# State delta of a chunked delta-rule attention kernel: 32-row parts of the turned keys in place of zero-padded key copies

## What is computed

```python
s = s * alpha[..., None]
u = jnp.einsum('bhd,bhdv->bhv', kt, s)
s = s - beta[..., None] * jnp.einsum('bhd,bhv->bhdv', kt, u)
s = s + beta[..., None] * jnp.einsum('bhd,bhv->bhdv', kt, vt)
out = jnp.einsum('bhdv,bhd->bhv', s, qt)
```

## Time and profile before

| | us |
|---|---|
| runs | 1864.84, 1876.25, 1890.15 |
| median of the runs | 1876.25 |
| the profiled execution's own time | 1873.82 |
| its span, first to last instruction | 1871.8 |
| PE busy | 1449.1 (77%) |
| DVE busy | 1274.1 (68%) |
| ACT busy | 634.8 (34%) |
| POOL busy | 360.1 (19%) |

### The profile page before, as it was taken

One profiled execution on the slowest core, in us unless ns is written; L12 is line 12 of the kernel. 1 busy time (PEld: TensorE's weight loads), 2 busy tenths in 40 slices (PEclk: granted clock), 3 DMA queues, 4 the chain that ended last, 5 costly groups with the idle time before them and its releaser, 6 DMA issues. The chain is left out here.

```text
span 1871.8 us, 46841 instructions
## 1 busy us (share of the span) xinstructions
PE 1449.1 (77%) x18540; PEld 946.9 (51%) x18568; DVE 1274.1 (68%) x3341; ACT 634.8 (34%) x1342; POOL 360.1 (19%) x515
## 2 busy tenths in 40 slices
PE   1687988797878887787879786888869897974685
PEld 0343664365525653465436562566436663652665
DVE  5568576966787667866796578765695678534564
ACT  4430243223422262134312352124312442222564
POOL 1210141014201320015101420023001420110232
PEclk8568996899689987998789979896699968996898
DMA  8980001010010001000100001000101000102223
GB/s 252 322 254 18 8 8 30 2 23 20 8 23 21 5 20 29 18 8 19 30 13 12 20 8 23 21 5 19 30 11 19 13 14 12 24 26 99 69 70 125
DMA packets 128139, 81.97 MB, mean 44 GB/s; under 512 B 75185, under 2 KB 118513, under 8 KB 127922
## 3 DMA queue, kind: packets, MB, share of 16 engines
q1 hardware_dynamic: 124466, 69.94, 13.6%
q0 software_dynamic: 3456, 8.95, 1.5%
HBM read 27.72 MB, written 51.15 MB: 42 GB/s over the span
## 5 line engine op out<-in xcount | busy, mean ns | idle before, releaser
L789 POOL COPY kx<-kend_t 32x256 f32<-32x256 f32 x256 | 114.3, 447 | 807.3 <-PE ps L1349 787.5
L1286 PE MATMUL ps<-wv,ident 128*128 128x512 f32 x320 | 173.7, 676 | 10.6 <-DVEq L1654 10.5
L1729 DVE SCALAR_TENSOR_TENSOR state<-state,gam,ps 128x128 f32<-128x128 f32 x512 | 137.4, 339 | 49.1 <-PE ps L1349 49.1
L1673 DVE TENSOR_TENSOR nv<-ps,nrm 128x512 f32<-128x512 f32 x64 | 44.2, 691 | 175.9 <-PE ps L1209 175.4
L1349 PE MATMUL ps<-w,kx 128*64 128x128 f32 x2048 | 127.1, 277 | 0.0
L1643 DVE TENSOR_TENSOR nv<-kq,kq_blk 128x31 f32<-128x31 f32 (+15 forms) x248 | 113.7, 458 | 16.7 <-ACT mem L852 10.8
L1349 PEld LDWEIGHTS ps<-w,kx 128*64 128x64 f32 x2048 | 111.7, 138 | 12.9 <-issue 12.9
L1521 DVE TENSOR_TENSOR kq_leaf<-kq,eleaf 128x1024 f32<-128x1024 f32 x32 | 39.9, 1247 | 112.6 <-ACT kq L882 112.4
L1286 PEld LDWEIGHTS ps<-wv,ident 128*128 128x128 f32 x320 | 66.7, 218 | 94.0 <-issue 77.5
L233 PE MATMUL ps<-eleaf,wf 128*128 128x512 f32 x112 | 62.0, 681 | 50.9 <-DVEq L1654 31.8
L999 ACT ACTIVATE w<-ps 128x512 f32<-128x512 f32 x64 | 38.2, 597 | 173.8 <-PE ps L1307 173.8
(11 more groups left out here) (313 smaller groups left out, 3303.9 us busy)
## 6 DMA issues: line engine op xcount, KB each, us to landing
slot_d<-row SPq DMA_DIRECT2D x16, 2064.0 KB, 20.3
xin<-slot_d SPq DMA_DIRECT2D x39, 129.0 KB, 2.1
a_d<-yt SPq DMA_DIRECT2D x8, 512.0 KB, 2.6
kq_blk<-a_d SPq DMA_DIRECT2D x32, 128.0 KB, 2.8
u_d<-kq SPq DMA_DIRECT2D x8, 512.0 KB, 2.6
ub<-u_d SPq DMA_DIRECT2D x128, 32.0 KB, 1.9
wall<-in_w SPq DMA_DIRECT2D x8, 512.0 KB, 7.9
xt<-in_xT POOLq DMA_DIRECT2D x8, 256.0 KB, 3.4
```

The source lines that it names most:

```text
L789: m = pool.tensor_copy(kx[part, :, b4, :], kend_t[part, g, 2 * q:2 * q + 2, :])
L1286: pe.matmul(bw.t[:, :], ident[:, :], wv[:, 0:512], start=True, stop=True)
L1729: k = dve.scalar_tensor_tensor(out=state[:, hp, b, :], in0=state[:, hp, b, :], scalar=gam[:, hp, b:b + 1], in1=bd[j].t[:, DV * x:DV * x + ...
```

## The change

The buffer `kx`, its clearing by ACT, its semaphore and the 256 copies by POOL are gone. PE multiplies 32 rows of `kend_t` by the same 32 rows of `w`: 16 products of 32 rows by 64 columns for each tile, in two halves. A half takes two sequences, which lie in two row groups of the array and go to the two banks; between the halves PE waits for `row_step`. The waits that went through `kx_ready` now name the delta banks: ACT's copy of `w` waits for both banks of the tile before, the overwriting of `kend_t` for the last tile of the chunk before, and POOL's `early_differences` for tile 5. POOL's body no longer waits for `xsum_ready`, which it had raised itself.

```diff
-    kx = sb("kx", [P, 2, GB, P])
...
@@ gpsimd body
-            for i in range(TILES):
-                g, q = i // 2, i % 2
-                if nxt and i == TILES - 1:
-                    pool.wait_ge(kx_ready.sem, kx_ready.at(c, TILES - 1))
-                    early_differences(nxt, c)
-                    pool.wait_ge(d_ready.sem, d_ready.at(nxt, 2))
...
-                for j in range(2):
-                    if i:
-                        pool.wait_ge(bd[j].full.sem, bd[j].filled(c, f"d{i - 1}"))
...
-                for b4 in range(GB):
-                    part = slice(CH * b4, CH * b4 + CH)
-                    m = pool.tensor_copy(kx[part, :, b4, :], kend_t[part, g, 2 * q:2 * q + 2, :])
-                m.then_inc(kx_ready.sem, 1)
+            for j in range(2):
+                pool.wait_ge(bd[j].full.sem, bd[j].filled(c, f"d{TILES - 3}"))
+            settle(c)
             if nxt:
-                pool.wait_ge(kx_ready.sem, kx_ready.at(c, TILES))
+                early_differences(nxt, c)
                 keep_h(nxt, c)
             if last:
-                pool.wait_ge(kx_ready.sem, kx_ready.at(c, TILES))
                 pool.wait_ge(zeroed, 16 * ZFILL)
                 head_on_pool(pool, last, room, "scatter", lambda: settle(c))
@@ scalar: ends_turned, body, first
-                act.wait_ge(kx_ready.sem, kx_ready.at(c, TILES, 1))
+                for j in range(2):
+                    act.wait_ge(bd[j].full.sem, bd[j].filled(c, f"d{TILES - 1}", 1))
...
-                        act.wait_ge(bd[1].full.sem, bd[1].filled(c, f"d{i - 1}"))
+                        for j in range(2):
+                            act.wait_ge(bd[j].full.sem, bd[j].filled(c, f"d{i - 1}"))
...
-            act.activation(kx[:, :, :, :].rearrange("p a b v -> p (a b v)"), zero(2 * GB * P),
-                           ACT.Copy).then_inc(s_cleared, 1)
@@ tensor body
-                    pe.wait_ge(kx_ready.sem, kx_ready.at(c, i + 1))
                     settle(c)
-                    for b4 in range(GB):
+                    for half in range(2):
+                        if half:
+                            m.then_inc(row_step, runs.next())
+                            pe.wait_ge(row_step, runs.n)
                         for j in range(2):
                             for h2 in range(2):
-                                o = DV * (2 * (b4 // 2) + j)
-                                m = pe.matmul(bd[b4 % 2].t[DK * h2:DK * h2 + DK, o:o + DV],
-                                              kx[:, j, b4, DK * h2:DK * h2 + DK], w[:, 2 * j + h2, :],
-                                              start=True, stop=True)
-                        if b4 >= 2:
-                            m.then_inc(bd[b4 % 2].full.sem, 1)
+                                for x in range(2):
+                                    b4, o = 2 * half + x, DV * (2 * half + j)
+                                    part, keys_of = slice(CH * b4, CH * b4 + CH), slice(DK * h2, DK * h2 + DK)
+                                    m = pe.matmul(bd[x].t[keys_of, o:o + DV], kend_t[part, g, 2 * q + j, keys_of],
+                                                  w[part, 2 * j + h2, :], start=True, stop=True)
+                                    if half and j and h2:
+                                        m.then_inc(bd[x].full.sem, 1)
```

More of the change, by code:

```diff
@@ L575, in attention @@
     row_step = sem("row_step")
-    pace, kx_ready = sig("pace", PACES), sig("kx_ready", TILES)
+    pace = sig("pace", PACES)
     beta_step, norm_step = sig("beta_step", 8), sig("norm_step", 7)
@@ L765, in body @@
                 head_on_pool(pool, last, room, "xsum", lambda: settle(c))
-            if last:
-                pool.wait_ge(hd.xsum_ready.sem, hd.xsum_ready.at(last, 1))
-            for i in range(TILES):
-                g, q = i // 2, i % 2
-                if nxt and i == TILES - 1:
-                    pool.wait_ge(kx_ready.sem, kx_ready.at(c, TILES - 1))
-                    early_differences(nxt, c)
-                    pool.wait_ge(d_ready.sem, d_ready.at(nxt, 2))
[L775 to L780, removed]
-                for j in range(2):
-                    if i:
-                        pool.wait_ge(bd[j].full.sem, bd[j].filled(c, f"d{i - 1}"))
-                    elif later(c):
-                        pool.wait_ge(bd[j].full.sem, bd[j].filled(c, f"d{TILES - 1}", 1))
-                settle(c)
-                for b4 in range(GB):
-                    part = slice(CH * b4, CH * b4 + CH)
-                    m = pool.tensor_copy(kx[part, :, b4, :], kend_t[part, g, 2 * q:2 * q + 2, :])
-                m.then_inc(kx_ready.sem, 1)
+            for j in range(2):
+                pool.wait_ge(bd[j].full.sem, bd[j].filled(c, f"d{TILES - 3}"))
+            settle(c)
             if nxt:
-                pool.wait_ge(kx_ready.sem, kx_ready.at(c, TILES))
+                early_differences(nxt, c)
                 keep_h(nxt, c)
             if last:
-                pool.wait_ge(kx_ready.sem, kx_ready.at(c, TILES))
                 pool.wait_ge(zeroed, 16 * ZFILL)
@@ L1370, in late @@
         def late():
-            pe.wait_ge(s_cleared, 3)
+            pe.wait_ge(s_cleared, 2)
             pe.wait_ge(s_late, n_late)
```

## The result

The changed kernel takes 1922.84 us (median of 4 runs, 1921.37 to 1924.24) beside 1874.6 for the kernel before (1864.84 to 1890.15): a ratio of 1.0249, 95% interval 1.0178 to 1.0321. It is slower by 48 us; 28 us less were forecast. The profiled execution took 1921.37 us with a span of 1919.7.

What follows compares the result with a forecast made beforehand. PE was taken to bound the tile loop, DVE most of the rest. 49.5 tiles x 0.57 = 28.2 us off 1873.82 left 1845.6, or 1848 from the runs' median; forecast 1847 us, range 1832 to 1880.

Steps and rivals of the forecast that it cites:

- the step from the delta to the sum: Tile loop: each tile's 0.57 us saving in the delta shifts all later PE work until PE waits for DVE.
- the sum of 49.5 tiles: Tile loops: 7 chunks x 6 tiles + 7.5 in the last chunk, each 0.57 us, together 28.2 us saved.
- The delta itself: PE's delta matmuls in each tile: 1.33 us instead of 1.90 to PE's next instruction, saving 0.57 us.
- The first rival: Delta: row groups take turns, 2.22 us instead of 1.90, 16 us lost, about 1890 us; chance 0.11.
- The estimate from TensorE: Matmul & The Clock Gate: Delta: a factor of 1.75 for two row groups gives 1.43 us, saving 0.47 a tile, 23 us in all.
- the rival of single products: Delta: all matmuls go singly, 107 ns each, so 3.8 us a delta and 1970 us in all; chance 0.03.
- What of it counts: Tile loop: six of eight tiles keep the 0.57 us, tiles 5 and 6 lose it; 7.5 count in the last chunk.
- the gain of tile 5: Tile 5's 0.57 us saving is lost, since PE then stands 1.68 us for `r` of tile 6.
- POOL: Dropping 114.3 us of copies is worth 0; early differences can start some 1 us earlier, nobody gaining.
- The second and third rival: DVE takes the gain, about 1861 or 1871 us, chance 0.13; all eight tiles count, about 1832 us, chance 0.13.

Runs made afterwards that it cites:

- The first two experiments: Kernel before with the delta in the changed order and with its new wait: 128-row products 1886.83 us; 32-row products, POOL's copies kept, 1936.7 us.
- the fourth: Changed kernel with every 32-row product of the delta done twice, writing the same values again: 1912.35 us.
- the first: Kernel before, padded copies and 128-row products kept, with the delta in the changed order and PE's new wait between halves: 1886.83 us.
- the tenth run: Kernel before plus unread products in the turns, before `w` of tile 6 and at the end of the chunk's body: 1877.09 us, ratio 1.0021.
- the eighth: Changed kernel plus unread products in the turns, before `w` of tile 6 and at the chunk body's end: 1861.2 us, again 1859.36 us.

## Why the prediction was wrong

**The step that failed** is the one from the delta to the sum: "so 0.57 shifts all that comes after, until PE waits for DVE", and with it the sum of 49.5 tiles. It took the granted clock of 1.00 in the tile loop as a property of the loop. It was one of the loop with the delta in it as it stood. With the delta shorter and on a quarter of the rows, PE's wait for `r` of tile 6, which the prediction had listed, and its waits for ScalarE in the turns, which it had not, were followed by stretches at the lower level. PE's work of the tile loop went from 68.3 to 72.6 us or more in the chunks of the hardware loop that are shown, although 0.55 us were gone from each tile, and these loops took 84 to 87 us, where 78.5 - 3.4 = 75.1 were forecast.

The first two experiments show that the lighter delta brings the falls, and neither PE's new wait inside it nor POOL; the filled runs show that the gain in the loops returns when the clock does. Of what makes the delta lighter, the rows have a part by themselves (the fourth against the first, one run each). What its shorter time does by itself, and what the longer waits that follow from it do, is not separated.

The prediction had read the clock in the loop, and had no rival in which it falls; its range ended at 1880. The page of the kernel before held a hint. Beside the solve PE already runs products that nobody reads, which the kernel calls `KEEP_WARM`:

```profile
L1286 PE MATMUL ps<-wv,ident 128*128 128x512 f32 x320 | 173.7, 676 | 10.6 <-DVEq L1654 10.5
```

**The delta itself** was right: 1.35 us against 1.33, 27 ns against "24 to 30", a wait of 0.35 against 0.36. The first rival, that the row groups take turns, is refuted. The trace agrees with the bank rule of the Trainium skill (TensorEngine Tiling (Array Packing), Restrictions and Gotchas) as far as it goes: two row groups with a bank each run side by side, at 27 ns; two in one bank no run tried. The estimate from TensorE: Matmul & The Clock Gate of the Trainium skill (Measured speedup vs the span model), 1.43 us, was too high by 0.08. In the rival of single products 107 ns should be 109, twice the 54.6 behind the 55; it changes nothing.

**What of it counts** was nearly right where the clock held: in the runs with unread products chunks at 1.00 are 78.50 - 75.50 = 3.0 us shorter than before, against 6 x 0.57 = 3.4, and the last 72.33 - 67.95 = 4.4, against 7.5 x 0.57 = 4.3. The missing 0.4 is tile 4. The prediction let its saving pass, but tile 4 stayed 13.1 us long: PE's wait for ACT in its turn grew by the 0.55 that the delta lost (1.29 to 1.84; from 0.86 in the tenth run to 1.41 in the eighth). Over the loops that makes 7 x 3.0 + 4.4 = 25 us at most; no run gave more than 24.8 (602.8 instead of 627.5), and in the time the best was 0.6%, not the 1.5% forecast. That the gain of tile 5 is lost to PE's wait for `r` came as said: the wait grew from 1.68 to 2.07 us.

**POOL** came as said: the copies were worth nothing, the early differences began 0.2 us after the last scan's end (665.45 after 665.27), about 1 us earlier than before, and nobody gained or lost by it that a run could show: the changed kernel and the one with parts and copies both stand at 0.81 to 0.86 in seven loops, and a smaller effect can't be told from one run. The second and third rival did not come.

## What to carry to other kernels

A matmul that is partly padding may be what keeps TensorE's clock up. Before work is taken from a dense stretch, look in the granted clock at the places where PE waits for another engine: if a stretch stands at 2.4 GHz with such waits in it, price it at 1.2 GHz from the rows that ran at that level (here up to twice the time, 6 us in a tile), and give that case a chance. If the clock falls, fill the waits with full-array products into a free bank: here six in the turns and two before one wait, in each chunk, took the ratio from 1.0249 to 0.998, level with the kernel before; the best of the runs came to 0.9937.

## What was not expected of the hardware

Doing the delta's products twice cost nothing in the tile loops: they took 664.5 us against 665.4, at a higher clock. PE's wait for `r` of tile 6 behind the lighter delta, 2.07 to 2.18 us, was followed by 17 to 20 us at 1.2 GHz in all seven chunks that have it; behind the padded delta, 1.67 to 1.78 us, by none in six of seven and by some 7 us in the other. And no set of unread products held the clock in all eight loops: each left falls at other places, in the first tile of the last chunk, in tile 4 or in the turn of tile 6. Why one such place falls and the next doesn't stays open.
